# Local attention in a three-part decoder layer: a new order of the projections in a turn, and GpSimd instructions cut into pieces

## The reference

```python
h = shift_token(x)
q, k, v = split(h @ wqkv, 3)                 # 8 heads of 64
q = l2norm(q) * qs;  k = l2norm(k) * ksc
q = q * cos * scale + rotate_half(q) * sin * scale
k = k * cos / scale + rotate_half(k) * sin / scale
sim = einsum(q * 8, k) over this block of 64 tokens and the one before
sim = where(i < j or i > j + 64, -max, sim)
o = softmax(sim) @ v
x = x + o @ wo
```

## Time and profile before

| | us |
|---|---|
| median of 3 runs | 2069.77 |
| lowest and highest run | 2054.02, 2069.95 |
| the profiled execution | 2067.86 |
| its span, first to last instruction | 2066.1 |

### The profile page before, as it was taken

The page is one execution under the profiler, slowest core; times in us unless marked ns, Lnnn a source line. Parts: engine busy times, 40 slices in busy tenths (PEclk is TensorE's granted clock), DMA queues, the critical chain, the costliest instruction groups (busy, mean ns, idle before and its releaser), DMA issues. The chain is left out here.

```text
span 2066.1 us, 67709 instructions
## 1 busy us (share of the span) xinstructions
PE 1786.4 (86%) x28076; PEld 1059.2 (51%) x28076; DVE 1089.7 (53%) x3240; ACT 1484.8 (72%) x2585; POOL 462.6 (22%) x351
## 2 busy tenths in 40 slices
PE   7987999999989999999986787777797687777788
PEld 4774555555555555555543455445432445544533
DVE  4455333333333333333126777777544877787654
ACT  4333999999989999999975676776533676767633
POOL 1004000000000000000007565555003655555200
PEclk9998999999999999999997999999898889999889
DMA  1002111111111111111020001000000000100000
GB/s 54 3 3 75 62 51 55 56 56 56 56 57 56 56 56 56 56 53 37 8 88 18 17 16 23 15 15 16 6 0 10 16 17 16 23 15 13 17 6 36
DMA packets 42327, 69.51 MB, mean 34 GB/s; under 512 B 7376, under 2 KB 33104, under 8 KB 42064
## 3 DMA queue, kind: packets, MB, share of 16 engines
q1 hardware_dynamic: 42064, 65.66, 10.1%
HBM read 21.08 MB, written 2.10 MB: 11 GB/s over the span
## 5 line engine op out<-in xcount | busy, mean ns | idle before, releaser
L653 ACT ACTIVATE x_probs<-x_pss 128x1024 f32<-128x1024 f32 x832 | 806.3, 1021 | 50.0 <-PE x_pss L574 35.0
L588 PE MATMUL x_acc<-x_probs,x_v 128*32 128x256 f32 x6656 | 437.3, 380 | 0.1
L574 PE MATMUL x_pss<-x_qx,x_kx 32*128 32x256 bf16 x9984 | 347.8, 270 | 13.8 <-issue 6.1
L574 PEld LDWEIGHTS x_pss<-x_qx,x_kx 32*128 32x128 bf16 x9984 | 221.2, 93 | 199.1 <-ACT x_probs L653 179.4
L588 PEld LDWEIGHTS x_acc<-x_probs,x_v 128*32 128x32 f32 x6656 | 206.4, 110 | 93.2 <-issue 9.0
L1182 ACT ACTIVATE l_prob<-l_sim,l_neg_top,l_inv_norm 128x128 f32<-128x128 f32 x512 | 245.2, 483 | 3.7 <-DVE l_neg_top L1086 3.7
L871 POOL TENSOR_TENSOR l_turned_half<-l_raw,l_tabB 128x512 f32<-128x512 f32 x128 | 195.7, 1550 | 168.4 <-ACT l_raw L1142 168.4
L700 DVE COPY x_vnext<-x_psp 128x128 f32<-128x128 f32 (+1 forms) x199 | 59.2, 298 | 315.3 <-PE x_psp L552 312.2
L967 PE MATMUL l_pst<-w_identity,l_prob 128*128 128x128 f32 x512 | 92.9, 310 | 135.2 <-DVE l_prob L1096 132.6
L880 POOL TENSOR_TENSOR l_direct<-l_direct,l_turned_half 128x1024 f32<-128x1024 f32 x64 | 151.5, 2368 | 146.9 <-DVE l_direct L1046 144.3
L916 PE MATMUL l_psqk<-w_wqkv,shifted 128*128 128x512 f32 x256 | 161.2, 764 | 26.8 <-ACT l_raw L1142 18.9
(11 more groups left out here) (166 smaller groups left out, 2684.8 us busy)
## 6 DMA issues: line engine op xcount, KB each, us to landing
x_kx<-x_kp SPq DMA_DIRECT2D x96, 208.0 KB, 2.3
x_cT<-in_context SPq DMA_DIRECT2D x16, 832.0 KB, 4.5
x_qx<-x_qp SPq DMA_DIRECT2D x48, 192.0 KB, 2.9
l_vmid<-l_vt SPq DMA_DIRECT2D x64, 128.0 KB, 2.3
xT<-in_x SPq DMA_DIRECT2D x8, 256.0 KB, 5.3
shifted<-zT SPq DMA_DIRECT2D x32, 64.0 KB, 2.0
out_x<-xT SPq DMA_DIRECT2D x8, 256.0 KB, 2.0
shifted<-zT SPq DMA_DIRECT2D x32, 63.8 KB, 2.0
```

Of the source, the lines that this page charges most:

```text
L574: ins = pe.matmul(pss[bank(k, 2 * p + r // 2)][:, r % 2, e, :], kx[par][rows, g, j * P:(j + 1) * P], qx[par][rows, g, a * S:(a + 1) * S], ...
L588: ins = pe.matmul(acc[32 * r:32 * r + 32, 0:S], v[:, j, g, r, :], probs[SLOT[p]][r // 2][:, r % 2, e, :], start=(u == 0), stop=(u == UNITS ...
L653: act.activation(probs[SLOT[p]][y][:, :, :, :], pss[bank(k, 2 * p + y)][:, :, :, :], ACT.Sigmoid, scale=HD ** -0.5).then_inc(weighed, 1)
```

## The change

It does four things. GpSimd's instructions are cut: turn_halves issues two for each half (four a tile, 256 columns each), join four of 256 columns a tile, scale_keys two of 256 columns a tile; the semaphore of a step is raised by its last piece (by the last of each half in turn_halves). TensorE's turn begins with project_v(x,0), and project_v(x,1) stands between the two turn_over steps; project_qk(x+2,1) follows ahead of value(x-1,1); project_out goes ahead of turn_over(x,0,0) and flip(x+1,1) ahead of turn_over(x,0,1). project_qk(x+2,1) gets a wait for mask(x,0,1), which keeps score(x,1) behind it. On VectorE copy_v(x,0) and copy_v(x,1) move up behind the two norms of x-1, place_keys(x+1,0) ahead of mask(x,1,0), and add(x-1) from the end of the turn to between norm(x,0,1) and mask(x,1,1).

```diff
--- before.py
+++ after.py
@@ -868,17 +868,23 @@
                     n, r, _ = x
                     pool.wait_ge(raw_ready, 2 * n + t + 1)
                     for lo, frm in ((0, FD // 2), (FD // 2, 0)):
-                        pool.tensor_tensor(heads(turned_half[t][:, :, lo:lo + FD // 2]),
-                                           heads(raw[t][:, :, frm:frm + FD // 2]),
-                                           table(tabB, t, lo, lo + FD // 2), ALU.mult).then_inc(halved, 1)
+                        for m in range(2):
+                            at = slice(m * FH, (m + 1) * FH)
+                            ins = pool.tensor_tensor(turned_half[t][:, at, lo:lo + FD // 2], raw[t][:, at, frm:frm + FD // 2],
+                                                     tabB[:, t, m, lo:lo + FD // 2].unsqueeze(1).broadcast_to([P, FH, FD // 2]),
+                                                     ALU.mult)
+                        ins.then_inc(halved, 1)
 
             def join(x, t):
                 if exists(x):
                     n, r, _ = x
                     pool.wait_ge(halved, (2 * n + t) * 2 + 2)
                     pool.wait_ge(straight, 2 * n + t + 1)
-                    pool.tensor_tensor(direct[r % 2][t][:, :, :], direct[r % 2][t][:, :, :], turned_half[t][:, :, :],
-                                       ALU.add).then_inc(joined, 1)
+                    for m in range(4):
+                        at = slice(4 * m, 4 * m + 4)
+                        ins = pool.tensor_tensor(direct[r % 2][t][:, at, :], direct[r % 2][t][:, at, :],
+                                                 turned_half[t][:, at, :], ALU.add)
+                    ins.then_inc(joined, 1)
 
             def scale_keys(x, t):
 
@@ -886,9 +892,11 @@
                     n, r, _ = x
                     pool.wait_ge(newton, 4 * n + 4)
                     pool.wait_ge(joined, 2 * n + t + 1)
-                    pool.tensor_tensor(direct[r % 2][t][:, FH:QK, :], direct[r % 2][t][:, FH:QK, :],
-                                       inv_norm[r % 2][:, t, FH:QK].unsqueeze(2).broadcast_to([P, FH, FD]),
-                                       ALU.mult).then_inc(scaled[t], 1)
+                    for lo in (FH, FH + FH // 2):
+                        at = slice(lo, lo + FH // 2)
+                        ins = pool.tensor_tensor(direct[r % 2][t][:, at, :], direct[r % 2][t][:, at, :],
+                                                 inv_norm[r % 2][:, t, at].unsqueeze(2).broadcast_to([P, FH // 2, FD]), ALU.mult)
+                    ins.then_inc(scaled[t], 1)
 
             def turn(x):
                 for t in range(2):
@@ -902,7 +910,9 @@
 
         @block.tensor
         def _(pe):
-            def project_qk(x, t):
+            def project_qk(x, t, scores_of=None):
+                if t == 1 and exists(scores_of):
+                    pe.wait_ge(masked, 4 * scores_of[0] + 2)
                 if exists(x):
                     n, r, q = x
                     if t == 0:
@@ -996,19 +1006,19 @@
                     ins.then_inc(out_ready, 1)
 
             def turn(x):
+                project_v(x, 0)
+                project_qk(later(x, 2), 0)
                 turn_over(later(x, -1), 1, 0)
-                project_qk(later(x, 2), 0)
+                project_v(x, 1)
                 turn_over(later(x, -1), 1, 1)
-                project_v(x, 0)
+                project_qk(later(x, 2), 1, x)
                 value(later(x, -1), 1)
-                project_qk(later(x, 2), 1)
-                project_v(x, 1)
                 score(x, 1)
                 flip(later(x, 1), 0)
+                project_out(later(x, -1))
                 turn_over(x, 0, 0)
-                project_out(later(x, -1))
+                flip(later(x, 1), 1)
                 turn_over(x, 0, 1)
-                flip(later(x, 1), 1)
                 value(x, 0)
                 score(later(x, 1), 0)
 
@@ -1105,23 +1115,23 @@
 
             def turn(x):
                 norm(later(x, -1), 1, 0)
+                copy_v(x, 0)
                 mask(x, 0, 0)
                 norm(later(x, -1), 1, 1)
+                copy_v(x, 1)
                 mask(x, 0, 1)
                 inverse_norms(later(x, 1))
-                copy_v(x, 0)
                 straight_part(later(x, 2), 0)
-                copy_v(x, 1)
                 sums(later(x, 2), 0)
                 norm(x, 0, 0)
+                place_keys(later(x, 1), 0)
                 mask(x, 1, 0)
-                place_keys(later(x, 1), 0)
                 norm(x, 0, 1)
+                add(later(x, -1))
                 mask(x, 1, 1)
                 place_keys(later(x, 1), 1)
                 straight_part(later(x, 2), 1)
                 sums(later(x, 2), 1)
-                add(later(x, -1))
                 floor_of(later(x, 2))
 
             for tab, const, scales in ((tabA, "cosine", "scales"), (tabB, "sine", "scales_turned")):
```

## The result

The changed kernel takes 2061.41 us (median of 20 runs, 2047.15 to 2072.13) against 2070.84 of the kernel before: ratio 0.9949, interval 0.9924 to 0.9973. That is 9.4 us less where the forecast of 2032 lies 39 us under the same median: the time is inside the range given (2004 to 2066), the gain a quarter of the one forecast. The profiled execution (2047.15 us, span 2045.4) is the fastest of the twenty.

A forecast was written before the change was run, and what follows sets the result against it. A loop of waits from turn to turn was taken to bound the kernel. 22.14 - 20.9 = 1.24 us a turn over 15 intervals in two layers, 37 us, gave 2031, and 1.9 for the median 2032 us; range 2004 to 2066.

The forecast's parts named there:

- The loop: Local-attention turn: a 12.5 us VectorE chain, then a 9.6 us ScalarE/TensorE chain, linked by the late value projection; 22.14 us.
- (b) the new order: project_v(x,0) first in TensorE's turn cuts the two chains apart; a turn takes 20.9 us at full clock.
- the sum: Both local-attention layers: 22.14 - 20.9 = 1.24 us a turn, 15 intervals in each layer, 37 us, giving 2032 us.
- The turn of 22.14: The one profiled turn of the kernel before in which TensorE kept its full clock, taken as base: 22.14 us.
- (a) the pieces: Smaller GpSimd instructions cap VectorE's waits at about 0.65 us, for 0 to 2.3 us more GpSimd work a turn.
- The part that doesn't shrink: Fixed cost of each further GpSimd piece when an instruction is cut: 0 to 0.19 us.
- Rival 4: Order frees nothing, only pieces count: floor's wait falls from 1.0 to about 0.3 us, 0.7 a turn; 2049 us, chance 0.03.
- the slacks: VectorE has 1.1 to 1.6 us to spare at three places of the new turn; a 0.65 us GpSimd wait fits each.
- (c) the clock: Turns of the two stages lose 0.79 us in the mean to TensorE's lowered clock; kept unchanged for the new order.
- rival 3: 1.2 GHz after both TensorE gaps in every turn: 24.4 us against 22.93, so 2113 us; chance 0.09.
- Fill and drain: Filling and draining turns of the local-attention stages: left as they are, no change counted.
- Signs: What would show it right (turns of 21 to 22 us) or wrong (22.5 or more, VectorE waiting at l_kT).

The follow-up runs named there:

- e1: Changed kernel with both idle gaps of TensorE filled by extra matmuls (before project_qk(.,1) and before value's second half); 2015.53 us, ratio 0.9738.
- e6: Changed kernel with only the first gap, ahead of project_qk(.,1), filled by extra matmuls; 2018.45 us, ratio 0.9783.
- e9: Kernel before with GpSimd's smaller pieces, old order, both of TensorE's longer gaps filled by extra matmuls; 2047.19 us, ratio 0.9908.
- e5: Kernel before with both of TensorE's longer gaps filled by extra matmuls; 2073.24 us, ratio 1.0038.
- e8: Changed kernel with GpSimd's old whole instructions (new order only), both gaps filled by extra matmuls; 2044.68 us, ratio 0.9909.
- e7: Changed kernel with only the second gap, before value's second half, filled by extra matmuls; 2016.31 us, ratio 0.9765.
- e2: Kernel before with only its long 2.8 us gap ahead of turn_over filled by 1280 columns of extra matmul; 2095.14 us, ratio 1.0137.

## Why the prediction was wrong

**The loop, and (b) the new order: right.** One loop through ScalarE and TensorE, 20.9 us at full clock: 20.51 in the changed kernel, 20.5 to 20.7 in e1 and e6. The gain at full clock is 22.14 - 20.51 = 1.6 us a turn, more than the 1.24 of the sum. The turn of 22.14 was one of the shorter ones: the six of the kernel before that hold no low clock average 22.34.

**(a) the pieces: price of a piece right, worth alone wrong.** The part that doesn't shrink is 2 x 0.729 - 1.272 = 0.186 us, and (4 x 0.727 - 2.352)/3 = 0.185 for the sums: the upper end of the range given. Rival 4's gain of 0.7 us a turn was read from one wait (the floor's). Measured at full clock: 0.3 (e9 beside e5). In the new order the pieces are worth 21.59 - 20.58 = 1.0 us (e8 beside e1): the slacks held with them and not without, as said.

**(c) the clock: this step failed.** "I keep 0.79" was kept between two bounds, with no reason taken from the new order. It carried a mean loss from a loop in which the slow project_qk had 1.1 us of ScalarE's work beside it into one in which project_qk(.,1), score and project_v have none. Over 26 turns of the profiled executions: before (22.84 + 23.07 - 2 x 22.14) x 13 = 21 us lost in 89 us at low clock, 0.24 us for each; after (22.19 + 21.60 - 2 x 20.51) x 13 = 36 us in 96, 0.38 for each. (With 22.34 as the full-clock turn of before its loss is 16 us, and the difference larger.) A turn loses 1.4 us, not 0.79, and it loses them to falls, since e1 has both gaps filled, 3 us at low clock and turns of 20.6 us. And the profiled execution is the luckiest: over the twenty the mean clock of the span goes from 0.945 (2047 us) to 0.930 (2072), about 1.8 us for each 0.001, correlation -0.95, with a median of 0.938, where 17 runs of before had 0.948. From 0.945 to 0.938 is another 13 us, or 0.4 a turn if all of it falls in the stages, which only the profiled execution could show: an estimate of 1.8 in all. With the full-clock turn at 20.51 the point of no gain, which rival 3 put at 2.0, lies at 22.93 - 20.51 = 2.4. What is left is 0.6 x 30 = 18 us, less the 6 of the next paragraph; 9.4 were measured, and the last few are open. Rival 3 had the mechanism and the two places (1.3 and 1.6 us against 1.6 to 1.8 and 1.7); its error was "in every turn": five of the 26 turns had no fall, and most of the others one.

**Fill and drain: left as they were, and not so.** The thirteen turns gained (22.84 - 22.19 + 23.07 - 21.60) x 13 = 27.6 us in the profiled executions, the two stages 777 - 756 = 21. The rest, 6 us, went back in the turns around them: the last two steps between middle copies take 21.4 and 15.7 us (22.8 and 15.7 in the second layer) where before has 20.8 and 13.4.

**Signs.** Of the signs named ahead, the turns of about 22 us and the waits for l_raw came. VectorE's wait for l_psvy is 1.1 us a turn (under 0.5 was said), ScalarE's share 0.72 and 0.74 (above 0.75), and the norm's mean 0.915 us (under 0.75). Of the signs of being wrong, VectorE does wait at l_kT (34.0 us in twelve turns), though without turns of 22.5 us, and the granted clock of the first layer's turns is 0.90.

## What to carry to other kernels

Price a fall of TensorE's clock by what stands beside the matmuls that it hits, not by the mean loss of the old order: an order that takes the cover from a projection pays for every fall. When a new order leaves idle gaps on TensorE, run it once with spare matmuls in a gap whose PSUM tile is free; here that turned a gain of 9 us into one of 51 (e7: 2016.31 us beside 2067.19, faster than both kernels). In the old order the filling of its longest gap made the kernel slower (e2), so each filling has to be measured. Cutting GpSimd's instructions shortens the longest wait of VectorE but makes waits more frequent, so it pays only where each wait has a slack that a piece fits into and the whole doesn't.

## What the runs showed of the hardware

- The clock fell after gaps of 1.8 us (e2), 2.5 (after) and 2.8 (before), but seldom in e7 with a gap of 2.5 in every turn when the other one was filled, and seldom in e6 with 1.7 us open. In the kernel before, TensorE stands idle 2.79 us ahead of turn_over in the turn of the earlier trace rows, whose project_qk keeps the clock, and as long one turn earlier, where project_qk is the slow one of the earlier trace rows. The length of one gap doesn't tell it.

```profile
1366.70 0.66 PE L967 MATMUL l_pst<-w_identity,l_prob 128*128 128x128 f32 x4 [2.79 <-DVE l_prob L1096]
```

- Each further piece of a GpSimd product by the sine table or of its sum costs 0.185 us, by the medians of whole and cut instructions.
- Everything outside the two stages took 1289 to 1303 us in the profiled executions though its code is the same: the first sigmoid of the cross attention starts at 209 to 222 us, and 38 to 65 us of the first 1075 are at low clock. So stage lengths, not whole spans, were compared where a few microseconds mattered.
